# A recurrent scan whose matmuls run on a guess of the state, with the state copied into the operand sets on GpSimd

## The reference, cut to what matters

```python
def step(h, xt):                                   # UGRNN cell, 256 steps, x: [8, 256, 128]
    m = concatenate([xt, h], -1) @ weight + bias   # weight [256, 256]
    g = sigmoid(m[:, :128] + 1.0)
    c = tanh(m[:, 128:])
    h_new = g * h + (1.0 - g) * c
    return (h_new, h_new)
x = x + swapaxes(lax.scan(step, cond, swapaxes(x, 0, 1))[1], 0, 1)
x = x + hyperbolic_transformer_block(x, t_emb=cond)  # adaLN, 16 heads of 8, FF 512
```

## Time and profile before

| | us |
|---|---|
| median of three runs | 462.44 |
| profiled execution, span from the first to the last instruction | 461.8 |
| from the first product of the scan (L1569) to the last | 280.5 |
| TensorE busy | 375.0 (81%) |
| VectorE busy | 304.8 (66%) |
| ScalarE busy | 231.7 (50%) |
| GpSimd busy | 78.5 (17%) |

### The profile page before, as it was taken

How to read it: one execution, slowest core, us unless ns; L and a number is a source line. 1 busy time by engine, 2 the same in 40 slices (tenths; PEclk the granted TensorE clock), 3 DMA queues, 4 the chain that set the end, 5 groups by cost and what they waited for, 6 DMA issues and landing times.

```text
span 461.8 us, 14117 instructions
## 1 busy us (share of the span) xinstructions
PE 375.0 (81%) x5296; PEld 253.9 (55%) x5296; DVE 304.8 (66%) x1938; ACT 231.7 (50%) x1025; POOL 78.5 (17%) x151
## 2 busy tenths in 40 slices
PE   1999899898857896857898999979599899778832
PEld 1755676566746675746666766636344446446510
DVE  5454444576777776777776676653842378699883
ACT  2123422325335425335446455645688878953952
POOL 7000000012000012000012000032210124266580
PEclk9999999999999999999999999985759989995966
DMA  7200840002000000000000000000000000000102
GB/s 179 62 1 4 181 95 3 2 3 48 1 1 3 1 4 1 2 2 1 2 3 3 1 4 1 2 2 2 3 2 3 1 2 4 1 2 1 23 1 68
DMA packets 9114, 8.42 MB, mean 18 GB/s; under 512 B 1276, under 2 KB 7694, under 8 KB 9047
## 3 DMA queue, kind: packets, MB, share of 16 engines
q1 hardware_dynamic: 8950, 7.26, 7.0%
q0 software_dynamic: 96, 0.26, 0.2%
HBM read 6.45 MB, written 1.08 MB: 16 GB/s over the span
## 4 chain that ended last, share of the span: by engine, by line
PE 56%; DVE 22%; ACT 12%; issue 5%; POOL 2%; DMA 1%; SPq 0%; DVEq 0%; ACTq 0%; POOLq 0%
PE zb L804 21%; PE tb L927 6%; PE zb L782 4%; DVE prod_hi L1569 4%; PE tb L751 4%; ACT state L1265 3%; PE firsts L1098 3%; PE firsts L983 2%; ACT prd L1421 2%; PE tb L898 2%; PE zb L1078 2%; PE firsts L967 2%; ACT state L1268 2%; PE zb L788 2%; PE firsts L804 2%
## 5 line engine op out<-in xcount | busy, mean ns | idle before, releaser
L804 PEld LDWEIGHTS zb<-prod_hi,whh 128*128 128x128 f16 x1920 | 73.7, 106 | 89.9 <-DVE prod_hi L1569 85.8
L1265 ACT ACTIVATE state<-zb 128x8 f32<-128x8 f32 x240 | 42.7, 178 | 152.9 <-PE zb L804 152.4
L804 PE MATMUL zb<-prod_hi,whh 128*128 128x8 f16 x1920 | 91.0, 171 | 34.7 <-DVE prod_hi L1569 34.0
L1569 DVE SCALAR_TENSOR_TENSOR prod_hi<-state 128x16 f16<-128x16 f32 x255 | 44.7, 175 | 83.0 <-ACT state L1268 80.1
L804 PE MATMUL zb<-prod_lo,whh 128*128 128x8 f16 x960 | 63.7, 172 | 0.0
L1575 DVE TENSOR_TENSOR prod_lo<-prod,prod_hi 128x16 f16<-128x16 f32 x255 | 44.7, 175 | 8.7
L1421 ACT ACTIVATE prd<-zb 128x640 f32<-128x640 f32 x64 | 42.2, 712 | 7.8 <-PE zb L1078 7.2
L804 PEld LDWEIGHTS zb<-prod_lo,whh 128*128 128x128 f16 x960 | 44.5, 107 | 0.8
L1571 DVE SCALAR_TENSOR_TENSOR prod<-state 128x16 f32<-128x16 f32 x256 | 43.3, 169 | 0.3 <-ACT state L1268 0.3
L1268 ACT ACTIVATE state<-zb 128x16 f32<-128x16 f32 x240 | 42.8, 178 | 0.0
L1577 DVE SCALAR_TENSOR_TENSOR state<-prod 128x8 f32<-128x8 f32 x256 | 40.8, 159 | 0.0
(11 more groups left out here) (378 smaller groups left out, 708.6 us busy)
## 6 DMA issues: line engine op xcount, KB each, us to landing
mod<-ada_rows SPq DMA_DIRECT2D x4, 768.0 KB, 11.8
resid<-in_x_dram SPq DMA_DIRECT2D x6, 128.0 KB, 3.7
ffz<-shift_rows SPq DMA_DIRECT2D x4, 131.0 KB, 3.3
out_dram<-state SPq DMA_DIRECT2D x8, 64.0 KB, 2.1
out_dram<-early SPq DMA_DIRECT2D x8, 64.0 KB, 2.1
yy<-in_L_cond_w_ada_dram SPq DMA_DIRECT2D x1, 384.0 KB
early<-in_L_cond_weight_dram SPq DMA_DIRECT2D x2, 128.0 KB
resid<-in_x_dram POOLq DMA_DIRECT2D x2, 128.0 KB, 3.5
```

Of the source, the lines that this page charges most:

```text
L804: i = pe.matmul(z_bank(t, k)[:, NB * (t % CH):NB * (t % CH) + NB], whh[:, half, p, k, :], src[:, NB * p:NB * p + NB], start=False, stop=Fa ...
L1265: act.activation(r[:, 24:32], z_bank(t, 1)[:, k:k + NB], ACT.Tanh, scale=-1.0 / ZS)
L1569: dve.scalar_tensor_tensor(prod_hi[:, :], r[:, 16:32], 1.0, r[:, 0:16], ALU.add, ALU.mult).then_inc(hi_ready, 1)
```

## The change

A step's state is now known twice. A guess of it comes first, made without the last correction; its fp16 form (`guessed`) feeds the high part of the next step's sums while the correction is still on its way. The exact state follows, and only the difference between it and the guess (`rest`, fp16) is multiplied afterwards. Both are made by the same two operations: one tanh of 32 outputs that puts candidate and gate into an operand set (`sets`), and one `tensor_tensor_scan` over 32 elements, which walks through four elements for each batch (-2; then candidate times that plus h; then gate times that plus h; then half of that plus candidate) and so computes the new state. Each of the two sets, one for the exact and one for the guess, needs the exact state of the step before in 16 places. GpSimd writes these, with two copies of 128 x 16 for each step.

So a step's queues are:

- TensorE: wait for `guess_in` and for `rest`; two matmuls with `rest`; wait for the guessed state; four matmuls with it into the next step's sums (before: twelve).
- ScalarE: tanh of the full sums; then tanh of the next step's high part alone, into the guess's set.
- VectorE: scan of the exact state (`h_row`), subtraction for `rest`; then wait for GpSimd's copies and for the guess's tanh; scan of the guess. Background work follows that.
- GpSimd: wait for the exact state, two copies; its background work now lies between the steps, at ticks.

Further: the state's rows are 32 wide and 192 of them are kept; the gate and candidate sums of a step lie in one bank, banks go by odd and even steps (so `first_x_part` and `x_part` go through parities); the bias of `ada` comes as a loaded block of 8 rows and is added on VectorE, in place of six matmuls on TensorE and four operations on ScalarE.

```diff
-SW = 24
+SW = 32
+SETW = 112
+KEPT = 192
@@ GpSimd
             def tokens(now):
+                yield from at_ticks(now, 16)
+                pool.wait_ge(load_rest, LOADS_REST)
+                pool.tensor_scalar(view(badab[:, D:D + 1], [3 * D, 2], [1, D]),
+                                   view(badab[:, D:D + 1], [3 * D, 2], [1, D]), 1.0, None,
+                                   ALU.add).then_inc(bada_in, 1)
+                yield from at_ticks(now, 62)
                 pool.wait_ge(mod_in, 64)
...
+            def step(t):
+                if t < STEPS - 1:
+                    pool.wait_ge(h_ready, t + 1)
+                    for n in range(2):
+                        i = pool.tensor_copy(view(sets[:, n, 1:2], [4, NB], [1, 2]), view(h_row(t)[:, 3:4], [4, NB], [0, 2]))
+                    i.then_inc(h_copied, 1)
-            run(lambda t: None, [tokens, *tails])
+            run(step, [tokens, *tails])
@@ TensorE
+            def z_part(t, k, half, h):
+                bank, i = z_cols(t)
+                return pe.matmul(bank[:, 256 * k + i:256 * k + i + NB], whh[:, half, k, :], h, start=False,
+                                 stop=False, skip_group_check=True)
+            def z_high(t):
+                pe.wait_ge(hi_ready, t + 1)
+                for k in range(2):
+                    for half in range(2):
+                        i = z_part(t, k, half, guessed_h(t - 1))
+                i.then_inc(part_z, 1)
+            z_high(0)
             def step(t):
-                pe.wait_ge(hi_ready, t + 1)
-                for k in (1, 0):
-                    for half in range(2):
-                        z_part(prod_hi, half, k, t)
+                if t < STEPS - 1:
+                    pe.wait_ge(guess_in, t + 1)
                 pe.wait_ge(lo_ready, t + 1)
-                z_part(prod_lo, 0, 1, t).then_inc(gate_z, 1)
-                z_part(prod_lo, 0, 0, t).then_inc(cand_z, 1)
+                z_part(t, 0, 0, rest[:, :])
+                z_part(t, 1, 0, rest[:, :]).then_inc(full_z, 1)
+                if t < STEPS - 1:
+                    z_high(t + 1)
@@ ScalarE
+            def tanhs(t, n):
+                bank, i = z_cols(t)
+                return act.activation(view(sets[:, n, 3:4], [39, 2], [38, 2], [4, NB]),
+                                      view(bank[:, i:i + 1], [256, 2], [0, 2], [1, NB]), ACT.Tanh, scale=1.0 / ZS)
+            def guess(t):
+                act.wait_ge(part_z, t + 1)
+                tanhs(t, 1).then_inc(guess_in, 1)
+            guess(0)
             def step(t):
-                act.activation(r[:, 24:32], z_bank(t, 1)[:, k:k + NB], ACT.Tanh, scale=-1.0 / ZS)
...
+                act.wait_ge(full_z, t + 1)
+                tanhs(t, 0).then_inc(tanh_in, 1)
+                if t + 1 < STEPS - 1:
+                    guess(t + 1)
@@ VectorE
+            def scan(dst, n):
+                return dve.tensor_tensor_scan(dst, *scan_terms(n), 0.0, ALU.mult, ALU.add)
+            def guess(t):
+                if t:
+                    dve.wait_ge(h_copied, t)
+                dve.wait_ge(guess_in, t + 1)
+                scan(guessed[:, t % 2, :], 1).then_inc(hi_ready, 1)
+            guess(0)
             def step(t):
-                dve.wait_ge(step_in, 2 * t + 1)
...
+                dve.wait_ge(tanh_in, t + 1)
+                scan(h_row(t), 0).then_inc(h_ready, 1)
                 if t < STEPS - 1:
+                    dve.wait_ge(h_ready, t + 1)
+                    dve.tensor_tensor(rest[:, :], view(h_row(t)[:, 3:4], [4, NB]),
+                                      guessed_h(t), ALU.subtract).then_inc(lo_ready, 1)
+                if t + 1 < STEPS - 1:
+                    guess(t + 1)
             def prepare(now):
...
+                yield from at_ticks(now, 22)
+                dve.wait_ge(ada_ps, 1)
+                dve.wait_ge(bada_in, 1)
+                for q in range(4):
+                    cols = slice(192 * q, 192 * q + 192)
+                    i = dve.tensor_tensor(ada[:, cols], tb[0:NB, q // 2, 192 * (q % 2):192 * (q % 2) + 192],
+                                          badab[:, cols], ALU.add)
```

More of the change, by code:

```diff
@@ L224, in ugrnn_block_kernel @@
         resid = sb("resid", [P, NT, D])
[L225 removed]
+        state = sb("state", [P, KEPT * SW])
+        sets = sb("sets", [P, 2, SETW])
         xT = sb("xT", [P, STEPS * NB])
@@ L244, in ugrnn_block_kernel @@
         condT = sb("condT", [P, NB])
-        prod = sb("prod", [P, 2 * NB])
-        prod_hi = sb("prod_hi", [P, 2 * NB], F16)
-        prod_lo = sb("prod_lo", [P, 2 * NB], F16)
+        guessed = sb("guessed", [P, 2, SW], F16)
+        rest = sb("rest", [P, NB], F16)
         yy = sb("yy", [P, NJ + 2, 3 * D])
@@ new lines, in first_x_part @@
+                n = NB * FIRST // 2
+                for par in range(2):
+                    bank = z_cols(par)[0]
+                    for k in range(2):
+                        z = bank[:, 256 * k:256 * k + n]
+                        pe.matmul(z, w0s[:, k, :], view(xT[:, NB * par:NB * par + 1], [2 * NB, FIRST // 2], [1, NB]),
+                                  start=(k == 0), stop=False, skip_group_check=True)
+                        for half in range(2):
+                            pe.matmul(z, b0h[:, half, k, :], onesh[:, 0:n], start=False, stop=False,
+                                      skip_group_check=True)
@@ new lines, in x_part @@
+            def x_part(c):
+                first = FIRST if c == 0 else 0
+                n = (CH - first) // 4
+                for par in range(2):
+                    for k in range(2):
+                        for q in range(2):
+                            t = CH * c + first + 2 * n * q + par
+                            if c and par == 0 and k == 0 and q == 0:
+                                pe.wait_ge(xT_sb, c + 1)
+                            i = 256 * k + z_cols(t)[1]
+                            pe.matmul(zb[:, c % 2, par, i:i + NB * n], w0s[:, k, :],
+                                      view(xT[:, NB * t:NB * t + 1], [2 * NB, n], [1, NB]),
+                                      start=(k == 0 and q == 0), stop=False, skip_group_check=True)
+                            yield
+                        i = 256 * k + NB * first // 2
+                        for half in range(2):
+                            pe.matmul(zb[:, c % 2, par, i:256 * k + 256], b0h[:, half, k, :],
+                                      onesh[:, 0:256 * k + 256 - i], start=False, stop=False,
+                                      skip_group_check=True)
@@ L820, in prepare @@
                 yield from x_part(0)
-                yield from at_ticks(now, 12)
+                yield from at_ticks(now, 15)
                 pe.wait_ge(load_rest, LOADS_REST)
@@ L1550, in _ @@
             dve.tensor_tensor(b0h[:, 1], b0s[:, :, :], b0h[:, 0], ALU.subtract).then_inc(x_split, 1)
-            settled(dve.tensor_copy(whh[:, 0], whs[:, :, :, :]))
-            dve.tensor_tensor(whh[:, 1], whs[:, :, :, :], whh[:, 0], ALU.subtract).then_inc(w_split, 1)
-            done_(dve.memset(prod[:, NB:2 * NB], 0.0))
+            settled(dve.tensor_copy(whh[:, 0], whs[:, :, :]))
+            dve.tensor_tensor(whh[:, 1], whs[:, :, :], whh[:, 0], ALU.subtract).then_inc(w_split, 1)
+            for first, value in ((0, -2.0), (40, 0.0), (43, 0.5)):
+                done_(dve.memset(view(sets[:, 0, first:first + 1], [SETW, 2], [4, NB]), value))
@@ L1555, in _ @@
             dve.wait_ge(condT_sb, 2)
-            settled(dve.tensor_scalar(prod[:, 0:NB], state[:, 0:NB], 2.0, None, ALU.mult))
-            done_(dve.tensor_copy(prod_hi[:, :], prod[:, :]))
-            settle()
-            dve.tensor_tensor(prod_lo[:, :], prod[:, :], prod_hi[:, :], ALU.subtract)\
-                .then_inc(lo_ready, 1)
+            h0 = view(sets[:, 0, 1:2], [4, NB])
+            settled(dve.tensor_copy(guessed_h(-1), h0))
+            dve.tensor_tensor(rest[:, :], h0, guessed_h(-1), ALU.subtract).then_inc(lo_ready, 1)
```

112 lines of the change are left out of this document (36 added, 76 removed).

## The result

| | before | after |
|---|---|---|
| median, us | 462.42 | 501.63 (4 runs, 500.95 to 502.96) |
| ratio | 1 | 1.0849 [1.0825, 1.0873] |
| span of the profiled execution, us | 461.8 | 499.2 |
| scan, 255 intervals, us | 281.8 | 320.1 |
| a step with nothing late, us | 1.067 | 1.133 |

The kernel became 8.5% slower. The scan holds the loss: from the first exact scan to the last it now takes 320.1 us, where the same 255 intervals took 281.8 (the 280.5 of the prediction are 254 of them), +38.3. The first step begins at 15.36 and not at 13.95, +1.4, and what follows the scan is 2.3 shorter; together the 37.4 between the two spans. The spans of repeated runs of either kernel differ by 2 us, so I read nothing into that last term.

What follows compares the result with a forecast made beforehand. The scan, one serial loop through three engines, was taken as the bound: 287.1 + 8.7 + 11.0 = 306.8 us against 280.5, +26.3; with 2.2 more, span 490.3, median 490.9 us, range 464 to 518.

Steps and rivals of the forecast that it cites:

- base, nothing late: Scan steps held by the two-step loop through GpSimd's copies and the guess: 0.9975 us a step, 0.07 shorter than before.
- GpSimd's pieces: GpSimd's background between pairs of copies delays the next copies and exact scan: 3.7 us a chunk, 11.0 in all.
- Loop A: Exact state to exact state in one step: scan, `rest`, two matmuls, tanh and handovers, 0.905 us.
- quiet steps: Scan steps without background, forecast near 1.0 us; the prediction counted as wrong if they were not.
- The long scan instruction: Rival, 16%: the scan instruction takes 2.0 ns an element, 0.033 us more each, giving 504 us.
- VectorE's order: In VectorE's queue the next exact scan can't start before 0.84 us plus that step's background, behind the wait for GpSimd.
- GpSimd's copies: GpSimd's two copies a step take 0.21 us each, one after the other, 0.42 for the pair.
- break-even pair: With GpSimd's pair of copies at 0.28 us, 0.14 a copy, the kernel's time would not change.
- TensorE's and ScalarE's background: Their background between scan steps stays at the earlier 8.7 us, bounds 0 and 17.
- The lock-out: Rival, 10%: GpSimd's copies wait for `rest` on VectorE to end and start 0.10 us late, +20.7, 511 us.
- The start: Ahead of the first step: +1.3 us for `first_x_part`, +0.35 for the first guess, 0.26 back from fewer weight operations.

Runs made afterwards that it cites:

- the moved wait: In the changed kernel, the wait for `hi_ready` moved from ahead of the exact scan to ahead of `rest`: 501.16 us, 1.0825.
- the single semaphores: Changed kernel with one semaphore for both scans: 493.89 us; then also one for TensorE's two waits, one GpSimd copy and two of three pieces split: 469.78 us.

## Why the prediction was right, and where it was not

The forecast was 490.9 us and the time 501.63, inside the range of 464 to 518, on the side that held most of the chance. The mechanisms it named are there, but the terms are off in both directions, the base by +35.5 us and the background by -22.2, and that the sum came so near is in good part luck:

| term | forecast | after |
|---|---|---|
| base, nothing late (254 intervals; 255), us | 253.4 | 288.9 |
| all background but GpSimd's pieces | 33.7 + 8.7 = 42.4 | 23.8 |
| GpSimd's pieces | 11.0 | 7.4 |
| sum | 306.8 | 320.1 |

*Loop A is the step that failed.* It was put at 0.905 and is 1.133, and the prediction's own test, quiet steps near 1.0, came out wrong. The pieces of the 0.228: the tanh of 32 outputs 227 ns and not 190, +0.037; the scan 223 and not 190, +0.033; `rest` +0.007; two matmuls 0.26 and not 0.25, +0.01; the handover to TensorE 0.11 and not 0.055; that from ScalarE 0.10 and not 0.03. That is 0.21; the rest is rounding. The last two are 0.125 together, more than half. I took handovers from the earlier trace rows as properties of the engine pair. They depend on the waits ahead of the instruction: the moved wait took 0.07 with it to `rest`, the single semaphores took the floor from 1.13 to 1.06 and then to 1.00. The diff showed both pairs of waits (`hi_ready` then `tanh_in` ahead of the exact scan, `guess_in` then `lo_ready` ahead of `rest`'s matmuls), and I costed the early one of each at nothing. The guess's scan has two waits as well, and there nothing was right: the late one is written first.

*The long scan instruction.* This rival, at 16%, is what the trace shows for the instruction: 223 to 226 ns for 32 elements, exactly its 0.19 + 0.033. The Trainium skill (page "DVE: opcode table, instruction layouts, handler registers and perf-mode slots", section Datapath and trigger behaviour) has `tensor_tensor_scan` at half throughput, and the trace fits it as far as one size can tell: the 0.033 over my estimate is 1.0 ns for each of 32 elements. The tanh of 32 outputs is as far over its estimate, so the excess alone doesn't prove the cause. Its 504 us is nearer to the time than my 490.9, but not for its reason alone: it put the extra time into VectorE's order, and the time is in loop A.

*GpSimd's copies.* 198 ns each, inside my 0.17 to 0.25 and by the nearest rows, but the second starts 0.14 behind the first, so the pair is 0.34 and not 0.42. It starts 0.06 behind the exact scan and not 0.09. That GpSimd starts one after the other was read from operations of which each needs the last; these two don't. A 128 x 32 copy takes 217 ns, so a copy is almost all fixed cost.

*VectorE's order.* Forecast 0.84 plus background. In the step shown above it is 1.12 with a background instruction of 0.40: 0.66 to the guess, 0.14 to the next instruction, 0.32 for it. So the fixed part is 0.80, and the background weighs 0.32. With loop A at 1.133 that is no longer than the step is anyway. That is why the surplus was not 33.7 us: the floor that I had too low took it over. The slope fell with it, 17 us per 0.10 upward against 20.7, and 8 downward. The break-even pair of 0.28 us was wrong outright: a pair at 0.22 (one copy) is still 6% slower, since loop A doesn't have the copies in it.

*TensorE's and ScalarE's background.* Left at 8.7 us, within bounds of 0 and 17. The classes of steps say that this was low: steps that have background on TensorE and VectorE went from 1.131 to 1.273 (47 steps), with ScalarE's too from 1.159 to 1.353 (49), while those with TensorE's alone (1.149) are 0.02 over the floor and those with VectorE's alone (1.190) 0.06, both with medians at the floor (1.133 and 1.134). The sign fits a hole on TensorE that is shorter than the pieces laid into it, with VectorE's background taking what slack was left. No run changed TensorE's background alone, so this is argued from the means and not shown.

*GpSimd's pieces.* The mechanism is as drawn, the size 2.45 us a chunk and not 3.7. Of the three stalls that I foretold at over 1 us, the first is 1.1 to 1.2 and the two others 0.5 to 0.7.

*The lock-out.* It had 10%, and it has no part in the change's time, but not for the reason that I gave. In the change VectorE's background stands behind the copies, so hardly any copy has a long VectorE instruction beside it (one of 510 is over 0.25 us). `rest` has: it runs from 38.20 and GpSimd's pair from 38.22, and the pair is 0.34, 0.33 at 105.74 with no VectorE instruction beside it. A first copy beside `rest` takes 203 ns, one alone 193, and `rest` takes 0.17 with GpSimd's queue empty too (the copy on VectorE, 38.86). In the run with the guess behind the background the same copies end 0.06 behind a VectorE instruction of 0.42, 68 times. The Trainium skill (page "SBUF — State Buffer", section Who interferes with whom) says that a VectorE instruction with two SBUF inputs contends with a GpSimd one that reads SBUF, and that run agrees. Beside `rest` a hold would hardly show, for `rest` ends 0.14 behind the copy's start, and a copy that then needs 0.06 more is as long as a free one. My price of 0.10 for it, copies that begin only when `rest` has ended, was wrong.

*The start.* +1.4 us to the first step where 1.3 + 0.35 - 0.26 was forecast: right.

## What to carry to other kernels

In a loop through several engines, look at the waits ahead of each instruction on the loop, and at their order, not only at the events. Where two waits stood ahead of an instruction and the one written last was the last to end, the handover was 0.06 to 0.07 us longer; where the one written first was the last to end (the guess's scan, TensorE with the copy on ScalarE), it was as short as with one wait. One counter that both producers step removed the cost. No run swaps two waits, so that writing the late wait first would do as well is an inference from these handovers, and the cheaper thing to try first. Shortening a serial loop by speculation makes a second loop of nearly the same length, and background that used to cost next to nothing then has no hole to stand in; price the background against the shorter of the new holes before the loop's own gain. And read a price for independent instructions from independent instructions: the start-to-start distance (0.14 for GpSimd's copies, 0.14 behind a scan) is what counts in a queue, not the duration.

## What was not expected of the hardware

- Two waits ahead of an instruction, the one written last ending last: 0.07 us more on VectorE (handover 0.10 against 0.03, `rest` 0.33 against 0.26 behind the scan), 0.06 on TensorE (0.115 against 0.053). The one written first ending last: nothing more (0.034 behind the copies on VectorE, 0.051 on TensorE with the copy on ScalarE). The same scan of the guess went from 0.034 to 0.100 when its last event came from the wait written last.
- A tanh with 32 outputs and a strided target takes 227 ns where 16 outputs took 0.18 and 204 took 0.374: not on the line between them.
- GpSimd's independent copies overlap: 198 ns each, 0.14 to 0.15 from start to start, and 217 ns for twice the elements in one.
- A GpSimd copy beside a VectorE instruction with two inputs in SBUF is held until 0.06 us behind that one's end (0.39 us and not 0.19 beside 0.42); beside one with an input in PSUM it isn't.
